# Sums by destination in a graph kernel: slot results in two pairs of PSUM banks, placement one step ahead of the additions, picked rows in SBUF

## What is computed

```python
edge_index = jnp.stack([src, dst])
x = _layernorm(x + _L0_gnn_ref(x, edge_attr_16, ...), axis=-1)
x = _layernorm(x + _L1_gnn_ref(x, edge_index, ...), axis=-1)
x = _layernorm(x + _L2_gnn_ref(x, edge_index, ...), axis=-1)   # agg = segment_sum(x[src], dst), twice
x = _layernorm(x + _L3_gnn_ref(x, src, dst, edge_type_8, ...), axis=-1)
# L3: msg = einsum('emh,eh->em', edge_emb[edge_type], x[src]); m = segment_sum(msg, dst); then a GRU step
```

## Time and profile before

| what | value |
|---|---|
| median of 3 runs | 5447.12 us (5445.19 to 5455.07) |
| the profiled execution, its time and its span | 5444.44 us, 5442.6 us |
| pass 0, first gather to the load behind it | 3104.2 to 3630.9 us |
| pass 1 | 3735.6 to 4265.5 us |
| pass 2 | 4512.6 to 5141.2 us |
| VectorE busy in the span | 3795.1 us (70%) |
| TensorE busy | 3274.5 us (60%) |
| GpSimd busy | 3080.9 us (57%) |

### The profile page before, as it was taken

How to read it: one execution, slowest core, us unless ns; L and a number is a source line. 1 busy time by engine, 2 the same in 40 slices (tenths; PEclk the granted TensorE clock), 3 DMA queues, 4 the chain that set the end, 5 groups by cost and what they waited for, 6 DMA issues and landing times.

```text
span 5442.6 us, 56112 instructions
## 1 busy us (share of the span) xinstructions
PE 3274.5 (60%) x12161; PEld 2405.8 (44%) x12161; DVE 3795.1 (70%) x6342; ACT 1641.6 (30%) x4066; POOL 3080.9 (57%) x2659
## 2 busy tenths in 40 slices
PE   5888888888614333333787534454444444876586
PEld 2444444444414333333666434443344324776432
DVE  5999999999776444443999845654556675555588
ACT  2555555555432111111333201111111341222143
POOL 2677776777603777776555577734777106777000
PEclk9999999999995555556998755667566565567698
DMA  3111111111152333332111100022000230000122
GB/s 92 31 38 38 37 35 35 38 38 35 33 149 52 52 52 52 52 44 34 48 47 42 33 7 7 7 71 77 7 7 7 84 99 12 7 7 7 31 84 74
DMA packets 407366, 231.38 MB, mean 43 GB/s; under 512 B 127146, under 2 KB 372078, under 8 KB 407234
## 3 DMA queue, kind: packets, MB, share of 16 engines
q1 hardware_dynamic: 287954, 210.36, 13.7%
q0 software_dynamic: 119296, 19.68, 6.6%
HBM read 152.10 MB, written 58.47 MB: 39 GB/s over the span
## 4 chain that ended last, share of the span: by engine, by line
POOL 31%; DVE 28%; issue 19%; DMA 9%; PE 8%; ACT 2%; SPq 1%; DVEq 1%; POOLq 0%; ACTq 0%
POOL extra L655 18%; POOL sums L639 8%; DMA sums<-cmb,sidx 5%; DVE arena L1590 5%; POOL xg L619 3%; PE ps L1074 2%; DVE arena L1312 2%; DVE arena L1336 2%; DVE arena L1532 2%; PE ps L983 2%; POOL ft_t L608 2%; DMA edge_in<-far_row 2%; DVE ps L1306 1%; DVE arena L1320 1%; DVE st L1368 1%
## 5 line engine op out<-in xcount | busy, mean ns | idle before, releaser
L1074 PE MATMUL ps<-arena 128*128 128x128 f32 x2976 | 681.1, 421 | 735.6 <-DVE arena L1515 663.2
L655 POOL DMA_INDIRECT extra<-x_t,srci x784 | 778.3, 993 | 527.6 <-issue 527.6
L1074 PEld LDWEIGHTS ps<-arena 128*128 128x128 f32 x2976 | 632.5, 323 | 776.7 <-issue 776.7
L639 POOL DMA_INDIRECT sums<-cmb,sidx x392 | 614.5, 1568 | 428.1 <-ACT cmb L770 206.8
L983 PE MATMUL ps<-edge_in,wl 17*128 17x512 f32 x784 | 704.4, 1076 | 67.2 <-DMA edge_in<-far_row 65.0
L1532 DVE TENSOR_TENSOR arena<-arena,ps 128x128 f32 x1488 | 428.0, 288 | 366.5 <-PE ps L1074 187.7
L619 POOL DMA_INDIRECT xg<-in_x,xidx x392 | 472.6, 1206 | 317.9 <-DVE xp L1294 197.8
L1021 PE MATMUL ps<-arena 128*128 128x128 f32 x992 | 227.4, 422 | 601.8 <-DVE arena L1399 601.8
L608 POOL DMA_INDIRECT ft_t<-fts,fidx x392 | 507.6, 1295 | 139.4 <-issue 117.8
L655 POOL DMA_INDIRECT extra<-h_t,srci x392 | 383.4, 978 | 248.1 <-issue 248.1
L821 ACT ACTIVATE ps<-extra 128x16 f32 x1488 | 171.2, 168 | 1065.8 <-SPq L572 868.7
(11 more groups left out here) (198 smaller groups left out, 6197.3 us busy)
## 6 DMA issues: line engine op xcount, KB each, us to landing
edge_in<-far_row SPq DMA_DIRECT2D x98, 256.0 KB
ain<-in_src_row SPq DMA_DIRECT2D x56, 448.0 KB, 3.9
xin<-x_t SPq DMA_DIRECT2D x42, 448.0 KB, 4.8
ain<-arena SPq DMA_DIRECT2D x42, 448.0 KB, 5.1
arena<-rel_t SPq DMA_DIRECT2D x63, 256.0 KB, 4.0
sums<-zero SPq DMA_DIRECT2D x88, 144.0 KB
x_t<-yout SPq DMA_DIRECT2D x28, 448.0 KB, 3.3
extra<-x_t,srci POOLq DMA_INDIRECT x784, 2.4
```

What stands on the lines that cost most here:

```text
L639: pool.indirect_dma_start(sums[t % TABLES], bass.IndirectOffsetOnAxis(ap=sidx[n % 2][:, j:j + 1], axis=0), cmb[n % 2][:, j, :], None, comp ...
L655: pool.indirect_dma_start(dy[:, t, :], None, table, bass.IndirectOffsetOnAxis(ap=srci[:, t:t + 1], axis=0)).then_inc(d_gathered[n % QUEUE] ...
L1074: last = pe.matmul(ps[2][:, j * P:(j + 1) * P], oneh[b][:, j * P:(j + 1) * P], placed[b][:, j * P:(j + 1) * P], start=True, stop=True)
```

## The change

1. `ysl` moves from PSUM to SBUF, to two free pieces of `extra`. ScalarE's `pick` now writes SBUF, and VectorE's `place` has both inputs in SBUF.
2. The slot products go alternately to `ps[2]` and `ps[3]` (two banks each). The products of step n wait for the additions of step n-2 and not n-1.
3. VectorE's order in a step is place(n+1), [place_types(n+3)], one_hot(n+2), collect(n). Ahead of the first step stand one_hot(0), place(0), one_hot(1).

No instruction is added or taken away as a whole; TensorE's, ScalarE's, GpSimd's and SyncE's orders stay as they are.

```diff
--- before.py
+++ after.py
@@ -249,8 +249,9 @@
                           for k, a in enumerate((6, 7)))
 
         ps = [ctx.enter_context(nc.psum_tensor(f"ps{k}", [P, 1024], FP32)) for k in range(4)]
-        ysl = [ps[3][:, 512 * b:512 * b + P] for b in range(2)]
+        ysl = [extra[:, 7 * UNIT + (1 + b) * P:7 * UNIT + (2 + b) * P] for b in range(2)]
         msg, io_p = ps[1][:, 0:P], ps[1][:, 512:512 + P]
+        slot_sums = [ps[2], ps[3]]
 
         block = ctx.enter_context(nc.Block())
 
@@ -1067,11 +1068,11 @@
                     pe.wait_ge(oneh_done, 2 * i + base + c + 1)
                     pe.wait_ge(placed_done, 2 * i + base + c + 1)
                     for h in range(2):
-                        if later(i, c, 1) or k:
-                            pe.wait_ge(acc_done, 2 * SG * i + SG * (base + c - 1) + SG // 2 * (h + 1)
-                                       + ACC_ZEROS * (k + later(i, c, 1)))
+                        if later(i, c, 2) or k:
+                            pe.wait_ge(acc_done, 2 * SG * i + SG * (base + c - 2) + SG // 2 * (h + 1)
+                                       + ACC_ZEROS * (k + later(i, c, 2)))
                         for j in range(SG // 2 * h, SG // 2 * (h + 1)):
-                            last = pe.matmul(ps[2][:, j * P:(j + 1) * P], oneh[b][:, j * P:(j + 1) * P],
+                            last = pe.matmul(slot_sums[b][:, j * P:(j + 1) * P], oneh[b][:, j * P:(j + 1) * P],
                                              placed[b][:, j * P:(j + 1) * P], start=True, stop=True)
                         last.then_inc(slot_ps, 1)
 
@@ -1510,6 +1511,8 @@
                                       ALU.is_equal).then_inc(oneh_done, 1)
 
                 def place(i, c):
+                    if not inside(i, c, SLOT_GROUPS):
+                        return
                     b = c % 2
                     dve.wait_ge(y_copied, 2 * i + base + c + 1)
                     dve.tensor_tensor(
@@ -1529,19 +1532,21 @@
                             dve.wait_ge(slot_ps, 4 * i + 2 * (base + c) + j // (SG // 2) + 1)
                         dve.wait_ge(acc_done, 2 * SG * i + SG * (base + c) + j + ACC_ZEROS * (k + 1))
                         o = acc[:, bass.ds(at[j], P)]
-                        dve.tensor_tensor(o, o, ps[2][:, j * P:(j + 1) * P], ALU.add).then_inc(acc_done, 1)
+                        dve.tensor_tensor(o, o, slot_sums[c % 2][:, j * P:(j + 1) * P], ALU.add).then_inc(acc_done, 1)
 
                 def step(i, c):
-                    place(i, c)
+                    place(i, c + 1)
                     if typed:
                         place_types(c + 3)
-                    one_hot(i, c + 1)
+                    one_hot(i, c + 2)
                     collect(i, c)
 
                 if typed:
                     for g in range(3):
                         place_types(g)
                 one_hot(0, 0)
+                place(0, 0)
+                one_hot(0, 1)
                 if typed:
                     for n in range(SLOT_GROUPS):
                         step(0, n)
```

## The result

The changed kernel takes **5532.4 us** (median of 4 runs, 5531.1 to 5538.5), the kernel before 5447.2 in the same comparison: a ratio of **1.0156, 95% interval 1.0138 to 1.0173**, some 85 us slower. The prediction was 5540. The profiled run is 5533.14 us, 88.7 more than the one of before.

What follows compares the result with a forecast made beforehand. GpSimd's gathers by destination were taken to set the pace; passes 0, 1 and 2 at +39, +36 and +18 us, together +93 on the profiled 5444.4, gave 5537, and 2.7 for the runs' median 5540 us; range 5490 to 5590.

Steps and rivals of the forecast that it cites:

- The hold: A gather beginning while VectorE runs an operation with two SBUF inputs ends 0.82 us behind that operation's end, delaying later gathers.
- The lead that I put at 0.03 us: How far a place must start ahead of a gather to hold it: some 0.03 us.
- Pass 0: First pass by destination: gathers 41 us longer from holds, 2 us gained at the end, +39 us.
- the share that is held: Passes 0 and 1: three in four third gathers behind a group's last held, 0.95 us each, 35 us for 49 groups.
- The added 0.04 for the copies: ScalarE's copy into SBUF takes 0.04 us longer, so the place starts 3.46 to 3.77 us behind the group's last gather.
- the upper bound of 57 us: Passes 0 and 1: most that the gathers of a pass grow, if all are held.
- Pass 1: Second pass by destination: gathers 41 us longer from holds, 5 us gained at the end, +36 us.
- Pass 2: Third pass by destination: 36 us of holds (place 23, place_types 13), 18 us gained at the end, +18 us.
- The chain: Pass 2's new wait of the place for turn, messages and pick: 9.9 or 11.0 us between place_types, covered by the gathers.
- B: Rival: no hold at all, only the gains at the ends, 5427 us; chance 0.12.
- C: Rival: no hold; pass 2's chain bounds at TensorE's lower clock, 10.7 us on average, 5446 us; chance 0.08.
- A: Rival: holds mostly missed, the place starting 0.05 us later, behind the third gather; 5488 us, chance 0.10.

Runs made afterwards that it cites:

- experiment 1: Changed kernel with the picked rows of passes 0 and 1 back in PSUM (`ps[0]`): 5446.4 us, ratio 1.0008.
- 2: Kernel before with only the picked rows moved to SBUF in all passes, old order, one pair of banks: 5549.2 us, ratio 1.0201.
- 4: Kernel before with the one-hot reading `io_8` in SBUF in place of its PSUM copy: 5553.1 us, ratio 1.0209.
- 3: Changed kernel with ten ScalarE copies per step, not eight, in passes 0 and 1, so the place starts later: 5481.7 us, ratio 1.0075.
- 5: Changed kernel with sixteen ScalarE copies per step, not eight, in passes 0 and 1: 5525.9 us, ratio 1.0146.
- experiment 7: Changed kernel with picked rows in PSUM in all passes and pass 2's products in `ps[2]` alone, place still ahead: 5441.0 us, ratio 0.9994.
- experiment 8: Changed kernel with PSUM rows in passes 0 and 1; pass 2 as in the kernel before until step 45, as changed from step 46: 5420.8 us, ratio 0.9953.
- experiment 6: Kernel before with products of passes 0 and 1 alternating between `ps[2]` and `ps[3]`, rows in `ps[0]`, old order: 5444.5 us, ratio 0.9999.

## Why the prediction was right

**The hold.** Right as forecast: it is the place with two SBUF inputs (experiments 1 and 2), the one-hot does it as well when both its inputs lie there (4), a held gather ends 0.82 behind the operation, and the order of the starts decides (3, 5). One of the rows on which it rested could not carry it: the gather "beside the place of today" starts only 0.02 us behind the place, so it would have gone free with two SBUF inputs as well. What carries it is the count. In passes 0 and 1 of the kernel before 106 gathers start from 0.045 us behind a place's start to 0.12 ahead of its end, and none took over 0.956 us. The lead that I put at 0.03 us is 0.045: in passes 0 and 1 of the changed kernel 21 gathers start 0.045 us or less behind a place or up to 0.06 ahead of it and take 0.95 at most, while the 29 that start from 0.045 to 0.10 behind one all take 1.94 to 2.00.

**Pass 0: +47.4 for +39.** The term that was too small is the share that is held. I took starts from 3.46 to 3.77 behind the group's last gather, evenly spread, and three quarters held at 0.95. In the trace, 8 places in 10 of those that start behind a landing lie between 3.56 and 3.71 and none comes behind the third gather. Of these 47 places five led the third gather by 0.03 us or less, and the other 42 held it. The added 0.04 for the copies was right (eight take 0.953 us, 0.917 before), but the spread was read from two rows that were near its ends. The 42 third gathers lost 41.0 us, where 35 was forecast for them; the 12 others lost 6.9, for 6.5. The gain at the end was 0.6 us, not 2.

Two smaller slips of the forecast changed nothing. In the kernel before, 26 of 62 places wait for ScalarE, and only 13 steps share a group; the other 23 places come late because VectorE, at 6.9 us a step, has fallen behind in the second half of the pass. The forecast lets one place of each group start on a landing, and that holds for the changed kernel all the same, since its steps are shorter: 48 places wait. And the upper bound of 57 us doesn't follow from 0.95 a hold, which gives 53 with all 49 held.

**Pass 1: +34.0 for +36.** The middle of the starts is 3.67 here, 0.03 us later than in pass 0, and 6 places come behind the third gather: 29 third gathers are held, not 42. Where the decision hangs on hundredths of a microsecond, two passes of the same code differ by 10 us. The shift is there before the place: ScalarE's first copy starts 2.53 us behind the group's last gather in pass 0 and 2.56 in pass 1 (medians). What shifts that I have not found. Of the tail, 4.2 were gained for 5 forecast.

**Pass 2: +12.5 for +18.** The gathers grew by 30.2, not 36: the place's holds were 38 for 26.8 us (23 forecast), those of place_types 38 for 14.8 (2 more lost 0.1 together), so that they grew by 3.2, where I had 13. I had forecast that an arbitrary moment of place_types would double its share; in fact it was 0.39 per hold. The trace shows why. 29 of the 49 place_types start within 0.5 us of the end of a place (in the last one the place starts at 5136.27 and place_types at 5137.66). They hold a gather in 28 cases, but for 5.3 us in all, 0.19 each: the gather that the place has held is out by then, and the next starts late in place_types. The 20 others hold ten, for 9.5 us, 0.95 each. It is the effect of experiment 4, two operations behind each other costing little more than one. The end was 94.0 us for 94, steps 5.47 for 5.46.

**The chain.** A place in pass 2 waits for the messages of its own group, as the forecast has it (the kernel's description has step n wait for group n+1). The forecast had it covered, ending with the gathers or just ahead. It is covered as far as time goes (experiment 7), with half of the place_types held up by it.

**The sum.** +93.9 in the passes for +93: the errors of +8.4, -2.0 and -5.5 nearly cancel. The forecast of each pass was right to 9 us, and the exactness of the total is luck.

**The rivals.** B falls with the held gathers of the changed kernel, which experiment 1 takes away with one operand. With it falls, for gathers like these, the inference of the Trainium skill (SBUF — State Buffer, section Who interferes with whom) that such an operation does not stall the generation of descriptors: here a gather's 0.94 us became 1.89, and 392 gathers took 48 us more. The other half of the page's rule, that two SBUF inputs contend with a GpSimd instruction that reads SBUF, agrees with the runs: a gather here takes its row numbers from `srci` in SBUF. No run had the row numbers elsewhere, so that this read is the cause is not shown. C was not seen: with the hold of the place gone (experiment 7) the groups were 10.48 us apart on average, not 10.7, and holds explain them. A was the nearest miss in mechanism; 0.2 us later starts make it true (experiment 3).

## What to carry to other kernels

Where GpSimd issues indirect transfers at its own pace and that pace bounds the stage, look at VectorE's long operations beside it and count those with both inputs in SBUF: each can hold one transfer until 0.8 us behind its own end, and an operand in PSUM avoids it. What a hold costs is read from the order of the two starts, not from overlap or busy shares: take the distribution of starts from many rows, since 0.1 us decides. A restructuring that frees the engine behind a bound stage pays only at the stage's end, so apply it there and leave the bounded part alone (22 us of shorter tails here, in experiment 8).

This kernel itself has more of the same, in a phase that no run touched. In the softmax phase of the kernel before, L1320 (one operand in PSUM) and L1328 (all in SBUF) follow each other, with a gather under each:

```profile
599.80 1.21 DVE L1320 TENSOR_TENSOR arena<-ps,arena 128x1024 f32<-128x1024 f32 x1
599.91 0.95 POOL L619 DMA_INDIRECT xg<-in_x,xidx  x1 [0.30 <-issue]
...
600.93 1.22 DVE L1328 SCALAR_TENSOR_TENSOR arena<-arena 128x1024 f32<-128x1024 f32 x1
601.16 1.81 POOL L619 DMA_INDIRECT xg<-in_x,xidx  x1 [0.30 <-issue]
```

Of the 784 gathers and scatters of L619 and L608, 251 start well inside (0.06 us behind the start to 0.15 ahead of the end) one of the operations L1328, L1332, L1336 and L1344, whose inputs all lie in SBUF; 248 of them take over 1.03 us, 211 us in sum beyond 0.984 each, the median of L608. 266 start as well inside L1306, L1312, L1318 or L1320, which have an operand in PSUM, and none takes over 0.991. What of the 211 us a change of operands would bring back is not shown, since no run tried it.

## What the runs showed of the hardware that I had not expected

- More work on ScalarE made the kernel faster: two more copies per step took some 44 us off (ratio 1.0075 for 1.0156), and six more on top gave 39 back (1.0146).
- Two operations with SBUF inputs back to back cost one hold of 1.0 us, not two (experiment 4); with 0.2 to 0.5 us between them the second adds 0.19 (pass 2 of the changed kernel).
- The holds by place_types in pass 2 vary from run to run with unchanged code in that pass: 11.6 us in the profiled run of before, 15.3 in experiment 6; in experiment 8, where that stretch is as before too, 21.2. That is near 0.2% of the kernel. The phases outside the passes vary by 14 us (experiment 8), and the two together are what an experiment here can't tell. I have no cause for either.
- How sharp the decision is: 0.045 us of lead for VectorE's operation, and the gather's time doubles, from 0.95 at most to 1.94 at least, with nothing between. (A gather that starts later in the operation is held too, but for less, since the end is what is fixed.) In passes 0 and 1 of experiments 2 and 3 it is the same: none held up to 0.042, all from 0.052 on.
